# Two attention heads' score tiles computed as one pair in the two halves of TensorE's rows

## The reference

```python
xn = group_norm(x, g1, beta1)
q, k, v = split(einsum('oc,bchw->bohw', w_qkv, xn), 3)     # each (B, 8 heads, hd=16, N=1024)
attn = einsum('bhdi,bhdj->bhij', q, k) * temp[None]        # (B, 8, 1024, 1024)
attn = softmax(attn, axis=-1)
out = einsum('bhdj,bhij->bhdi', v, attn)
```

## Time and profile before

| what | value |
|---|---|
| median of 3 runs | 2107.11 us (2105.62 to 2115.0) |
| span of the profiled execution | 2109.6 us |
| PE busy | 1830.4 us (87%), 7380 matmul instructions |
| PE weight loads (PEld) | 944.4 us (45%) |
| DVE busy | 1072.8 us (51%) |
| ACT busy | 870.3 us (41%) |
| POOL busy | 184.6 us (9%) |
| DMA engines' share | 8.7% hardware queue, 0.3% software queue |
| mean granted clock of TensorE | 0.918 of full speed |

### The profile page before, as it was taken

The page is one execution under the profiler, slowest core; times in us unless marked ns, Lnnn a source line. Parts: engine busy times, 40 slices in busy tenths (PEclk is TensorE's granted clock), DMA queues, the critical chain, the costliest instruction groups (busy, mean ns, idle before and its releaser), DMA issues.

```text
span 2109.6 us, 23070 instructions
## 1 busy us (share of the span) xinstructions
PE 1830.4 (87%) x7380; PEld 944.4 (45%) x7380; DVE 1072.8 (51%) x1941; ACT 870.3 (41%) x1530; POOL 184.6 (9%) x189
## 2 busy tenths in 40 slices
PE   6678679988998889988998889988998889888886
PEld 3344344455545454445444445454544344444332
DVE  4241584557445654547355663556554655554701
ACT  1022114444444444444344443444444444454562
POOL 5003002100110001100120001100020001100000
PEclk9789789999999999989899898999999989999997
DMA  2000102010101010010100101010100110011000
GB/s 45 10 10 1 30 1 40 1 31 1 31 21 31 1 21 12 21 31 1 32 21 14 18 2 30 21 31 1 31 10 13 19 24 7 11 31 31 10 1 10
DMA packets 19567, 37.35 MB, mean 18 GB/s; under 512 B 8742, under 2 KB 10990, under 8 KB 19440
## 3 DMA queue, kind: packets, MB, share of 16 engines
q1 hardware_dynamic: 18352, 35.21, 8.7%
q0 software_dynamic: 1088, 0.53, 0.3%
HBM read 5.98 MB, written 4.20 MB: 5 GB/s over the span
## 4 chain that ended last, share of the span: by engine, by line
PE 50%; issue 32%; DVE 11%; ACT 3%; SPq 2%; DMA 1%; POOL 1%; ACTq 0%; DVEq 0%; POOLq 0%
PE ps L970 50%; DVE mx L944 6%; DVE mx L880 1%; SPq L401 1%; ACT p L663 1%; DMA kp<-k3l 0%; POOL mv L478 0%; DVE mv L769 0%; ACT vT L597 0%; SPq L415 0%; DVE x L828 0%; DVE x L827 0%; DVE sg L842 0%; DVE pg L808 0%; ACT hn L584 0%
## 5 line engine op out<-in xcount | busy, mean ns | idle before, releaser
L944 DVE TENSOR_REDUCE mx<-ps 128x1 f32<-128x512 f32 x1024 | 674.4, 685 | 567.6 <-PE ps L970 565.2
L663 ACT ACTIVATE p<-ps 128x512 f32<-128x512 f32 x1024 | 592.5, 598 | 767.2 <-PE ps L970 754.0
L970 PE MATMUL ps<-kp,qp 112*128 112x512 f32 x1024 | 470.7, 478 | 99.4 <-DVE mx L944 81.8
L970 PE MATMUL ps<-qp,kp 128*128 128x512 f32 x1024 | 492.7, 500 | 54.4 <-ACT p L663 35.3
L970 PEld LDWEIGHTS ps<-kp,qp 112*128 112x128 f32 x1024 | 197.9, 195 | 307.9 <-DVE mx L944 228.4
L970 PEld LDWEIGHTS ps<-qp,kp 128*128 128x128 f32 x1024 | 200.0, 201 | 246.7 <-ACT p L663 142.3
L970 PE MATMUL ps<-p,vt 128*32 128x512 f32 x2048 | 282.9, 627 | 0.0
L500 POOL TENSOR_TENSOR acc<-acc,p 128x512 f32<-128x512 f32 x96 | 122.7, 1278 | 332.0 <-ACT p L613 332.0
L970 PE MATMUL ps<-p,vT 128*128 128x512 f32 x256 | 151.1, 675 | 0.0
L613 ACT ACTIVATE p<-ps 128x512 f32<-128x512 f32 x128 | 76.5, 598 | 131.0 <-PE ps L970 131.0
L478 POOL TENSOR_TENSOR mv<-mv,neg_half 128x1 f32<-128x1 f32 x24 | 13.2, 551 | 1079.1 <-DVE mv L779 1079.1
(11 more groups left out here) (200 smaller groups left out, 1701.1 us busy)
## 6 DMA issues: line engine op xcount, KB each, us to landing
qp<-q3h SPq DMA_DIRECT2D x128, 64.0 KB, 2.4
kp<-k3h SPq DMA_DIRECT2D x128, 64.0 KB, 2.4
xin<-in_x SPq DMA_DIRECT2D x8, 512.0 KB, 3.7
qp<-q3l SPq DMA_DIRECT2D x64, 64.0 KB, 2.4
kp<-k3l SPq DMA_DIRECT2D x64, 64.0 KB, 2.4
out<-p SPq DMA_DIRECT2D x8, 512.0 KB, 2.8
qp<-nm3T SPq DMA_DIRECT2D x64, 4.0 KB
p<-padded_taps POOLq DMA_DIRECT2D x32, 16.0 KB, 2.1
```

Source lines behind the costliest of these rows:

```text
L663: a.activation(p3[:, s % 2, i, :], ps[:, SB + p % 2, :], ACT.Exp).then_inc(sem("p3_ready"), 1)
L944: v.tensor_reduce(mx3[:, i, c, h:h + 1], ps[:, MB + n % 2, :], AX.X, ALU.max).then_inc(sem("mx3_ready"), 1)
L970: return nc.tensor.matmul(o, l, r, start=start, stop=stop)
```

## The change

`SPAN` = 64 and `PAIRS` (32 in a group) take the place of `ROWS` and `TILES`. Two heads, an even and an odd one, share a slot of `kp` as they did of `qp` (`kp` has four slots instead of eight). A pair of score tiles is two matmuls, one over rows 0 to 48 and one over rows 64 to 112, into banks SB and SB + 1. One exponential of 128x1024 covers both. A pair of maxima tiles is two matmuls over rows 0 to 47 and 64 to 111 into banks MB and MB + 1, and one reduction of 128x2x512 into 128x2. Each pair is released by the second matmul of it, and PE issues a pair once the reducer has finished the pair before it. Pairs are issued in even laps only. The product with v moves from the last lap of a step (i = 3) to the first lap of the next (i = 0), and so does the copy of `og`. The row of negated maxima is now the 49th of each half (rows 48 and 112), and the ones come from a memset of all of `kp` to 1.0; the memset of `qp` and the eight DMAs of ones are gone.

```diff
-ROWS = 64 + PACK
-TILES = GH * NC * NH
+SPAN = 64
+PAIRS = GH // 2 * NC * NH
-MAXIMA_TILES = ("00000020220320222011110001212211121100011212222220231001011110000000",
-                "00000002200222202200110212131120220112022031020220311200002020000000")
+MAXIMA_PAIRS = ("0000111211112111121111211112111000",
+                "0000111211112111121111211112111000")
 def maxima_at(g, p):
-    tiles = [int(n) for n in MAXIMA_TILES[g]]
-    first = sum(tiles[:p])
-    tiles = range(first, first + tiles[p])
-    return tiles[:1], tiles[1:]
+    if p % 2:
+        return (), ()
+    counts = [int(n) for n in MAXIMA_PAIRS[g]]
+    first = sum(counts[:p // 2])
+    pairs = range(first, first + counts[p // 2])
+    return pairs[:1], pairs[1:]
...
-        kp = sb("kp", [128, HEADS, N], F32R)
+        kp = sb("kp", [128, HEADS // 2, N], F32R)
...
-                sp.wait_ge(sem("ones_ready"), 1)
-                sp.wait_ge(sem("packs_zeroed"), 2)
-                for hd in range(HEADS):
-                    r = 126 + hd % 2
-                    sp.dma_start(raw(kp[r:r + 1, hd, :]).rearrange("p (a b) -> p a b", b=128),
-                                 raw(ones_r[0:NC, :])).then_inc(sem("k_ones_in"), 16)
+                sp.wait_ge(sem("k_ones"), 1)
...
-                                r = 126 + hd % 2
+                                r = SPAN * (hd % 2) + PACK
...
-                g.memset(raw(qp[:]), 0.0).then_inc(sem("packs_zeroed"), 1)
...
-                        if heads and s < STEPS:
+                        if heads and s < STEPS and i % 2 == 0:
                             step = g * STEPS + s
...
-                            u = g * TILES + p
-                            wait(act, sem("s3_ps"), bt, NG * TILES, u + 1)
-                            a.activation(p3[:, s % 2, i, :], ps[:, SB + p % 2, :], ACT.Exp).then_inc(sem("p3_ready"), 1)
-                        if heads and i == GH - 1 and s and s % NC == 0:
+                            u = g * PAIRS + p // 2
+                            wait(act, sem("s3_ps"), bt, NG * PAIRS, u + 1)
+                            a.activation(p3[:, s % 2, i:i + 2, :].rearrange("p a b -> p (a b)"), two(SB), ACT.Exp).then_inc(sem("p3_ready"), 1)
+                        if heads and i == 0 and s and s % NC == 0:
...
-                v.memset(raw(kp[:]), 0.0).then_inc(sem("packs_zeroed"), 1)
+                v.memset(raw(kp[:]), 1.0).then_inc(sem("k_ones"), 1)
...
-                v.tensor_reduce(mx3[:, i, c, h:h + 1], ps[:, MB + n % 2, :], AX.X, ALU.max).then_inc(sem("mx3_ready"), 1)
+                v.tensor_reduce(mx3[:, i:i + 2, c, h], ps[:, MB:MB + 2, :], AX.X, ALU.max).then_inc(sem("mx3_ready"), 1)
...
-                wait(pe, sem("mx3_ready"), mb, NG * TILES, mg * TILES + n - 1)
-                mm(ps[:, MB + n % 2, :], part(qp[0:ROWS, hd // 2, :], c), half(kp[0:ROWS, hd, :], hh)).then_inc(sem("s3max_ps"), 1)
+                wait(pe, sem("mx3_ready"), mb, NG * PAIRS, mg * PAIRS + n)
+                for e in range(2):
+                    rows = slice(SPAN * e, SPAN * e + PACK)
+                    last = mm(ps[:, MB + e, :], part(qp[rows, m, :], c), half(kp[rows, m, :], hh))
+                last.then_inc(sem("s3max_ps"), 1)
...
-                            wait(pe, sem("p3_ready"), bt, NG * TILES, u - 1)
-                            mm(ps[:, SB + p % 2, :], part(kp[:, hd, :], j), half(qp[:, hd // 2, :], h)).then_inc(sem("s3_ps"), 1)
+                            wait(pe, sem("p3_ready"), bt, NG * PAIRS, g * PAIRS + p // 2)
+                            for e in range(2):
+                                rows = slice(SPAN * e, SPAN * e + PACK + 1)
+                                last = mm(ps[:, SB + e, :], part(kp[rows, m, :], j), half(qp[rows, m, :], h))
+                            last.then_inc(sem("s3_ps"), 1)
...
-                        if heads and i == GH - 1 and s:
+                        if heads and i == 0 and s:
                             h, j = divmod(s - 1, NC)
...
-                            wait(pe, sem("p3_ready"), bt, NG * TILES, g * TILES + GH * s)
+                            wait(pe, sem("p3_ready"), bt, NG * PAIRS, g * PAIRS + GH // 2 * s)
```

More of the change, by code:

```diff
@@ L394, in pack @@
                 hd = GH * g + i
-                r, c = 64 * (hd % 2), HD * hd
+                r, c = SPAN * (hd % 2), HD * hd
                 if i == 0:
                     wait(sp, sem("vt3_ready"), bt, NG, g + 1)
-                for dst, parts in ((qp[:, hd // 2, :], (q3h, q3l, q3h)), (kp[:, hd, :], (k3h, k3h, k3l))):
+                for dst, parts in ((qp[:, hd // 2, :], (q3h, q3l, q3h)), (kp[:, hd // 2, :], (k3h, k3h, k3l))):
                     for n, part3 in enumerate(parts):
@@ L939, in largest @@
             def largest(n, mb, mg):
-                u = mg * TILES + n
-                wait(dve, sem("s3max_ps"), mb, NG * TILES, u + 1)
-                i, c, h = n // (NC * NH), n // NH % NC, n % NH
-                v.tensor_reduce(mx3[:, i, c, h:h + 1], ps[:, MB + n % 2, :], AX.X, ALU.max).then_inc(sem("mx3_ready"), 1)
+                u = mg * PAIRS + n
+                wait(dve, sem("s3max_ps"), mb, NG * PAIRS, u + 1)
+                i, c, h = 2 * (n // (NC * NH)), n // NH % NC, n % NH
+                v.tensor_reduce(mx3[:, i:i + 2, c, h], ps[:, MB:MB + 2, :], AX.X, ALU.max).then_inc(sem("mx3_ready"), 1)
             def passes(bt, sides):
@@ L954, in passes @@
                         if maxima and p == M_END:
-                            wait(dve, sem("mx3_ready"), mb, NG * TILES, (mg + 1) * TILES)
+                            wait(dve, sem("mx3_ready"), mb, NG * PAIRS, (mg + 1) * PAIRS)
                             v.tensor_reduce(nm3[:], mx3[:].rearrange("p i c h -> p (i c) h"), AX.X, ALU.max,
@@ L1240, in scores_in_rows @@
             def scores_in_rows(n, mb, mg):
-                hd, c, hh = GH * mg + n // (NC * NH), n // NH % NC, n % NH
-                if n % (2 * NC * NH) == 0:
-                    wait(pe, sem(f"packed{hd % GH // 2}"), mb, 16 * 12 * NG, 16 * 12 * (mg + 1))
+                m, c, hh = GH // 2 * mg + n // (NC * NH), n // NH % NC, n % NH
+                if n % (NC * NH) == 0:
+                    wait(pe, sem(f"packed{n // (NC * NH)}"), mb, 16 * 12 * NG, 16 * 12 * (mg + 1))
                 if n == 0:
                     wait(pe, sem("nm3T_ready"), mb, NG, mg)
-                wait(pe, sem("mx3_ready"), mb, NG * TILES, mg * TILES + n - 1)
-                mm(ps[:, MB + n % 2, :], part(qp[0:ROWS, hd // 2, :], c), half(kp[0:ROWS, hd, :], hh)).then_inc(sem("s3max_ps"), 1)
+                wait(pe, sem("mx3_ready"), mb, NG * PAIRS, mg * PAIRS + n)
[3 more added lines that the diff above has]
+                last.then_inc(sem("s3max_ps"), 1)
             def passes(bt, sides):
@@ L1256, in passes @@
                     pe.wait_ge(sem("wo_in"), 16 * HEADS)
-                    pe.wait_ge(sem("k_ones_in"), 16 * HEADS)
-                    pe.wait_ge(sem("packs_zeroed"), 2)
+                    pe.wait_ge(sem("k_ones"), 1)
                 heads = bt.exists()
@@ L1267, in passes @@
                         h, j = divmod(s, NC)
-                        if heads and s < STEPS:
-                            hd, u = GH * g + i, g * TILES + p
-                            wait(pe, sem("p3_ready"), bt, NG * TILES, u - 1)
-                            mm(ps[:, SB + p % 2, :], part(kp[:, hd, :], j), half(qp[:, hd // 2, :], h)).then_inc(sem("s3_ps"), 1)
+                        if heads and s < STEPS and i % 2 == 0:
+                            m = (GH * g + i) // 2
+                            wait(pe, sem("p3_ready"), bt, NG * PAIRS, g * PAIRS + p // 2)
[3 more added lines that the diff above has]
+                            last.then_inc(sem("s3_ps"), 1)
                         early, late = maxima_at(mg, p) if maxima else ((), ())
```

## The result

The changed kernel takes 2265.68 us (median of 6 runs, 2262.17 to 2288.88); the kernel before took 2109.74 us beside it. The ratio is 1.076 (95% interval 1.071 to 1.081): slower by 7.6%, outside the predicted range of 1995 to 2200 us.

The account below looks back on a forecast made before the run. PE's own work bounds most laps, the reducers some. Of 29.4 us saved an image, 13.5 go into shapes and 13.4 into waits; 21 us gained in 8 images, +3 for the last group, gives 2088 us, range 1995 to 2200.

Parts of the forecast that it names:

- Overlap in the two halves: On PE, the two half-row matmuls of a pair cost one matmul's 0.23 us: 236 us off, 29.4 an image.
- Rival D: The halves do not run side by side on PE: 0.46 us a pair, +123, 2230 us; chance 0.13.
- the 0.30 that I had named as a sign of being wrong: Sign on PE: the forecast is wrong if pairs cost 0.30 us or more.
- The reducers: For each pair, a maximum over 2x512 on DVE takes 1.22 us, an exponential of 1024 columns on ACT 1.02.
- Changes of shape: Switching the array's shape on PE costs 0.175 us; 77 more an image, 13.5 us, 108 in all.
- The waits: PE's minimum waits for the reducers cost 19.4 us an image instead of 6.0.
- walk: Sum over half-steps of the largest of PE work, score cycle and maxima: 197.4 us an image before, 194.8 after.
- A: The forecast: overlap, shapes and waits as priced, 2060 to 2117 us; sign, some 230 us of PE idle; chance 0.36.
- C: PE's waits for single-buffered pairs reach 47 us an image: 2239 us; signs, idle well over 300, image 259; chance 0.22.
- The clock: TensorE's mean clock stays near 0.92; 45 us an image outside the walk, half clock included, left unchanged.
- rival E: More short idle on PE doubles time at half clock: +124, 2212 us; sign, mean clock under 0.88; chance 0.08.
- The stages: In the last group a step of four scores takes 3.34 us instead of 3.15; 16 of these, +3 us.

Follow-up runs that it names:

- the stream: Loops of matmuls by themselves on one image of x, without the reference's computation; a half-row pair took 0.229 us, a change of shape 0.20.

## Why the prediction was wrong

- **Overlap in the two halves**: right. 0.229 us for a pair in the stream. Rival D falls. In the kernel a maxima pair starts 0.34 us behind the score pair ahead of it, which is past the 0.30 that I had named as a sign of being wrong; by the run that issues pairs twice it belongs to the change of shape.
- **The reducers**: right, 1.224 and 1.024 us against 1.22 and 1.02.
- **Changes of shape**: right in size. 0.20 us in the stream, 0.10 to 0.18 in the run that adds them, against 0.175. For the 600 more that the changed kernel has than the run with full-height pairs, that is 60 to 111 us; I had 108 for 616.
- **The waits**: right in steady state. By the same walk, full-height pairs have 12.5 us of waits an image where the kernel before has 6.0. With the 44.9 us that the walk leaves open in the kernel before (242.3 - 197.4) this makes 191.4 + 12.5 + 44.9 = 248.8 us for an image; the image at clock 0.95 took 249.7. In the changed kernel the visible idle, 217 us, was A's and not C's. Over the whole run, with images at a lower clock and with both ends, the walk was too low: pairing cost 141 us and not 52. 93 us of that are visible idle, and at 0.39 us each some 40 go with the 103 us more at half clock. The walk also took six half-steps of a group with two maxima pairs; the kernel has five.
- **The clock**: the step that failed, and with it the forecast: "the 45 us an image that the walk does not explain (half clock, ...) I leave as they are". They grew to 256.0 - 194.8 = 61.2. Those 16.3 us an image are what the clock's price gives: 0.85 over 256.0 us is 77 us at half clock, 0.93 over 242.3 was 34, and 43 x 0.39 = 17. The mean clock of the run went from 0.918 to 0.792, the sign named for rival E (under 0.88), which I gave 0.08. I reasoned there from idle time alone. But with the same pairs, waits and order at full height the clock was 0.900; with half rows 0.792 to 0.813; with half rows issued twice 0.843.
- **The stages**: the last group, priced at +3 us (3.34 for a step), took 4.50 for a step, +22 us. At full clock, with full-height pairs, it took 3.75. The first negation of maxima came 25 us later (336.4 us instead of 311.0), in a stretch whose clock was 0.63 where it had been 0.80.

These sum up, as an estimate, if all eight images lose what the steady ones do: 8 x 16.3 = 130, 25 at the start and 22 - 3 = 19 at the end, 174 of the 196 us by which the profiled execution (2287.1) missed its forecast (2091).

The other ledger goes from run to run: 2109 + 141 (pairs share their banks, with the fall of the clock that follows) = 2250. Then -236 (streaming), +60 to 111 (shapes), and the clock: it fell from 0.900 to 0.809 in a run of typical time (span 2260.4 us), so the time at half clock rose from 449 to 863 us, by 414. At 0.39 us each that is 161; with PE streaming in about 0.6 of an image, half of 0.6 would give 124. The sum lies between 2198 and 2286, and the kernel takes 2265. No run here switches the clock alone in the whole kernel, so its share stays an estimate; four measured steps (4.50 at half clock, 3.67 and 3.68 with filler, 3.75 at full height) show the effect by itself in one stage.

That the time came near rival C's 2239, and the image (256.0) near its 259, is luck: its waits did not come.

The Trainium skill, TensorEngine Tiling (Array Packing), Key Properties, whose drain between tiling modes stood against the change, is borne out here by a price for each change: 0.20 us in the stream, 0.10 to 0.18 in the kernel. What decided was bank sharing and the clock, though.

## What to carry to other kernels

Count a reduction's banks before its instructions: two tiles under one reduction halve the number of reductions in flight, and where PE issues in order behind such waits that cost 6 to 7% here, while neither reducer had been short of time. When small matmuls are packed side by side, look at the clock of the stages that wait: here a step with waits fell to half clock once packed, and everything else in it, the product with v above all, paid nearly double (1.93 us instead of 1.06). And a single pair of half-row matmuls amid full-height work cost 0.2 us on each side in the stream, more than the 0.23 that it saves; bunch them or leave them.

## What the runs showed of the hardware that I had not expected

- Single matmuls over 48 rows, back to back and without a gap, came behind a stream at full clock and ran at 0.50 (0.42 us each in that stretch); pairs of them, and full-height ones, ran at 1.00 (0.23). Matmuls over 112 rows, of which 48 hold data and the others zeros, left the kernel before at 0.918; cut to their 48 or 49 rows, with more changes of shape, they left it at 0.72.
- The same instructions took 249.7 us at a mean clock of 0.95 and 260.3 at 0.90, two images in a row of one execution. Before times of two kernels are compared, their clocks have to be.
- In a stage with waits, work that nobody needs made a step shorter: 4.50 us to 3.67 with 1.3 us of filler in it.
- Two half-row matmuls side by side took as long as one full-height matmul, 0.229 us (27.5 / 120 for pairs; 100 full-height ones from 57.88 to 80.80 us).
